# One message-passing kernel: who multiplies the first of four groups of edge values, ScalarE or VectorE

## The reference, cut to what matters

```
qi = Q[src]; kj = K[dst]
score = (qi * kj).sum(-1) + 0.1 * (edge_attr * qi[:, :RBF]).sum(-1) + logm[dst]
smax = segment_max(score, src)
es = exp(minimum(score - smax[src], 20.0))
denom = segment_sum(es, src)
alpha = es / (denom[src] + 1e-10)
m = h[dst] @ Wm[i]
aggi = segment_sum(alpha[:, None] * m, src)
```

## Time and profile before

| | us |
|---|---|
| median of 3 runs (5575.12, 5592.55, 5577.47) | 5577.47 |
| the profiled execution | 5589.14 |
| its span from the first to the last instruction | 5587.4 |
| around the span | 1.7 |
| `attend` in the third layer, from the first `keys` (3018.2) to the end of the last `total` (3445.6) | 427.4 |
| `attend` in the fourth layer (3545.5 to 3974.6) | 429.1 |

### The profile page before, as it was taken

The page is one execution under the profiler, slowest core; times in us unless marked ns, Lnnn a source line. Parts: engine busy times, 40 slices in busy tenths (PEclk is TensorE's granted clock), DMA queues, the critical chain, the costliest instruction groups (busy, mean ns, idle before and its releaser), DMA issues. The chain is left out here.

```text
span 5587.4 us, 187942 instructions
## 1 busy us (share of the span) xinstructions
PE 4125.9 (74%) x78491; PEld 3524.3 (63%) x78576; DVE 3831.4 (69%) x8933; ACT 2701.2 (48%) x8154; POOL 2683.2 (48%) x2702
## 2 busy tenths in 40 slices
PE   6888885026666489859976996799477844977886
PEld 4455553015555389849975996699456823977786
DVE  6888875149999689849966986699584446436254
ACT  3333331026666479839974996599402424100410
POOL 2777777757666267717762774377222500000000
PEclk7666665559999699969986997899697976988897
DMA  9322222248777366436634662566166342000000
GB/s 355 81 74 74 69 67 68 57 95 210 193 198 207 101 171 178 134 87 171 175 106 113 181 172 67 154 175 176 32 123 212 136 145 86 2 10 4 4 4 11
DMA packets 537236, 653.08 MB, mean 117 GB/s; under 512 B 321984, under 2 KB 369220, under 8 KB 533141
## 3 DMA queue, kind: packets, MB, share of 16 engines
q1 hardware_dynamic: 499989, 591.11, 38.0%
q0 software_dynamic: 33856, 48.44, 3.7%
q10 hardware_dynamic: 2496, 0.98, 0.1%
HBM read 460.24 MB, written 180.09 MB: 115 GB/s over the span
## 5 line engine op out<-in xcount | busy, mean ns | idle before, releaser
L299 POOL DMA_INDIRECT edges<-sb_bk_rec,sb_bk_pos x782 | 785.9, 1005 | 324.4 <-issue 234.1
L1749 ACT ACTIVATE sb_at_val<-banks,sb_at_prob 128x49 f32<-128x49 f32 x3800 | 783.0, 349 | 42.9 <-PE banks L1674 36.5
L1797 DVE CUSTOM_DVE_ANT_0 sb_at_left<-banks,sb_at_others 128x512 f32<-128x512 f32 x1000 | 644.9, 660 | 108.9 <-PE banks L1655 93.6
L1634 PE MATMUL banks<-sb_near,sb_at_hotT_d 128*128 128x49 bf16 x11100 | 617.8, 185 | 28.9 <-DVE sb_at_key L1774 10.6
L1636 PE MATMUL banks<-sb_queryp,sb_at_hotT_s 128*128 128x49 bf16 x11400 | 633.5, 186 | 5.6 <-issue 5.5
L1634 PEld LDWEIGHTS banks<-sb_near,sb_at_hotT_d 128*128 128x128 fp8e4 x11100 | 565.1, 97 | 35.9 <-issue 28.7
L1636 PEld LDWEIGHTS banks<-sb_queryp,sb_at_hotT_s 128*128 128x128 fp8e4 x11400 | 565.2, 96 | 6.7 <-issue 6.0
L1594 POOL TENSOR_TENSOR sb_at_key<-sb_at_key,sb_at_attr 128x400 f32<-128x400 f32 (+1 forms) x400 | 374.1, 936 | 371.9 <-ACT sb_at_key L1722 350.4
L1732 ACT ACTIVATE sb_at_others<-sb_at_hotT_s,sb_at_minus_big 128x1536 bf16<-128x1536 fp8e4 (+2 forms) x400 | 534.7, 1337 | 3.9 <-DVE sb_at_tops L1797 3.9
L1601 POOL TENSOR_TENSOR sb_at_val<-sb_at_val 128x490 f32<-128x490 f32 (+1 forms) x400 | 387.5, 969 | 67.3 <-ACT sb_at_val L1749 65.8
L1674 PE MATMUL banks<-sb_near,sb_at_hotT_d 128*128 128x49 bf16 x11100 | 364.6, 186 | 51.2 <-ACT sb_at_val L1749 32.2
(11 more groups left out here) (696 smaller groups left out, 10284.1 us busy)
## 6 DMA issues: line engine op xcount, KB each, us to landing
edges<-sb_pad SPq DMA_DIRECT2D x95, 460.0 KB, 7.2
sb_gt_rec<-edges SPq DMA_DIRECT2D x25, 1748.0 KB
sb_at_attr<-attr SPq DMA_DIRECT2D x100, 400.0 KB, 3.4
sb_at_attr<-attr SPq DMA_DIRECT2D x100, 360.0 KB, 4.0
sb_at_hot_s<-rows_src SPq DMA_DIRECT2D x100, 320.0 KB, 3.7
sb_we_hotT<-rows_dst_t SPq DMA_DIRECT2D x52, 592.0 KB, 5.8
sb_at_hotT_s<-rows_src_t SPq DMA_DIRECT2D x96, 320.0 KB, 3.3
sb_at_hotT_d<-rows_dst_t SPq DMA_DIRECT2D x96, 320.0 KB, 3.2
```

The lines of the kernel that those rows point to most:

```text
L299: pool.indirect_dma_start(list1, bass.IndirectOffsetOnAxis(pos[:, t:t + 1], 0), rec[:, k, j, :], None).then_inc(sent[k], 16)
L1634: pe.matmul(ps[:, 0, H1 * j:H1 * j + H1], where, what, start=(n == 0), stop=(n == 2))
L1749: ins = act.mul(val[:, v % VB, j, 0, :], ps[:, 5, H1 * j:H1 * j + H1], prob[:, i % 2, k:k + 1])
L1797: dve.tensor_tensor_reduce(left[:, x % 2, 0:n], ps[:, 3 + x % 2, 0:n], others[:, w % 2, ks[0] - first:ks[-1] + 1 - first, :].rearrange("p ...
```

## The change

A new helper on DVE weighs the first group of each block (10 slots) in one instruction, right before `scores` in the step in which ACT used to do it. ACT's `weigh` returns at once for q = 0. Since two engines now weigh, the count of weighed groups is held by two semaphores, and every wait for it becomes a helper, `weighed`, that waits for both: on PE ahead of every `values`, on POOL ahead of every `remainders`, on ACT ahead of the exponential.

```diff
+        def weighed(eng, v):
+            if v:
+                eng.wait_ge(s_val0, -(-v // Q))
+            if v - -(-v // Q):
+                eng.wait_ge(s_val, v - -(-v // Q))
...
             def remainders(v):
...
-                pool.wait_ge(s_val, v + 1)
+                weighed(pool, v + 1)
...
             def values(i, q):
                 v = Q * i + q
-                if v:
-                    pe.wait_ge(s_val, v)
+                weighed(pe, v)
...
             def weigh(i, q):
                 v = Q * i + q
                 if q == 0:
+                    return
+                if q == 1:
                     act.wait_ge(s_prob, i + 1)
...
+            def weigh(i):
+                v, n = Q * i, len(TAKE[0])
+                dve.wait_ge(s_prob, i + 1)
+                dve.wait_ge(s_h, v + 1)
+                if v >= VB:
+                    dve.wait_ge(s_sum, v - VB + 1)
+                dve.tensor_tensor(val[:, v % VB, 0:n, 0, :], ps[:, 5, 0:H1 * n].rearrange("p (j f) -> p j f", f=H1),
+                                  bc(prob[:, i % 2, 0:n], H1), ALU.mult).then_inc(s_val0, 1)
...
+                if 0 <= u - LAG - 1 < U and (u - LAG - 1) % Q == 0:
+                    weigh((u - LAG - 1) // Q)
                 if 1 <= u <= U:
                     scores(*divmod(u - 1, Q))
```

More of the change, by code:

```diff
@@ L1522, in attend @@
     names = ["keys", "rowk", "key", "dot", "score", "split", "turned", "rows", "laid", "top", "max", "mgot", "shift", "prob",
-             "h", "val", "rest", "split2", "sum", "added", "link", "minus", "others"]
+             "h", "val", "rest", "split2", "sum", "added", "link", "minus", "others", "val0"]
     rings = [f"attr{k}" for k in range(2)] + [f"hots{k}" for k in range(2)] + [f"hotT{k}" for k in range(HT)] + [
@@ L1528, in attend @@
             block, s_keys, s_rowk, s_key, s_dot, s_score, s_split, s_turned, s_rows, s_laid, s_top, s_max, s_mgot, s_shift,
-            s_prob, s_h, s_val, s_rest, s_split2, s_sum, s_added, s_link, s_minus, s_others, *dmas):
+            s_prob, s_h, s_val, s_rest, s_split2, s_sum, s_added, s_link, s_minus, s_others, s_val0, *dmas):
         s_attr, s_hots, s_hotT, s_far = dmas[0:2], dmas[2:4], dmas[4:4 + HT], dmas[4 + HT:8 + HT]
+        def weighed(eng, v):
[3 more added lines that the diff above has]
+                eng.wait_ge(s_val, v - -(-v // Q))
         @block.sync
@@ L1737, in probs @@
                 if i >= 2:
-                    act.wait_ge(s_val, Q * (i - 1))
+                    weighed(act, Q * (i - 1))
                 act.activation(prob[:, i % 2, :], shift[:], ACT.Exp).then_inc(s_prob, 1)
```

## The result

The changed kernel takes **5628.72 us** (median of 6 runs, 5615.97 to 5644.51), the kernel before in the same set of runs 5585.56 (5575.12 to 5592.55). The ratio is **1.0074, 95% interval [1.0057, 1.009]**: 41 us slower, with 32 to 50 as bounds (the two medians are 43 apart). The forecast was 5568.5 with a range to 5616; the measured time lies above that range. The kernel before came out 8 us higher in these six runs than in the three that the forecast started from, but 41 us on that lower base would give 5619, still above the range. In size the change is that of the rival "the race for the port is lost" with all 51 near ties turned (+38).

The account below looks back on a forecast made before the run. The order within one block (15.39 us), led by PE's unbroken run, was taken as the bound. -6 us from the drain and -3 from `values` gave -9, hence 5568.5 us; range 5553 to 5616, the forecast alone 5555 to 5583.

Parts of the forecast that it names:

- the race for the port is lost: Rival, chance 0.34: POOL takes the shared SBUF port before DVE's second divide instruction; +6 us (17 blocks) to +38 (51).
- near ties: 51 of 100 blocks where DVE's second divide instruction starts only 0.01 to 0.06 ahead of POOL's key addition.
- The chain of a block: From one `maxima` to the next: PE, ACT's key copy, POOL's addition, DVE's divide and tops; 15.39 us in most blocks.
- ten multiplications less on ACT: 2.03 us per block removed where ACT's next copy waits for PE anyway: worth 0 in mid-layer.
- the addition covered: DVE's added work fits into waits and 0.57 slack; the rival, not covered, costs 0.37 to 0.59 a block, chance 0.07.
- DVE's new instruction: 128x490 ahead of `scores`: 0.67, net 0.59 after overlap; delays the first divide instruction's start by 0.37.
- The price of `values`: In q = 3 PE no longer waits for ACT: 0.04 to 0.05 in some 60 of 100 blocks, about -3 us.
- few races lost: The forecast's own case, chance 0.48: change hidden but for the drain, POOL seldom first at the port.
- The price of a lost race: DVE's third divide instruction ends 0.86 later on the chain; such blocks last 16.2.
- The second waits: Second semaphore on 400 waits each of PE and POOL: 0 to 0.07 each, taken as 0.
- The drain: Behind a layer's last keys, PE waits less for ACT: 2.0 less 0.5 for waits, 1.5 a layer, -6 us in four.
- the first of the two savings: In the drain, `values` of group 93 waited 1.11 for ACT; DVE, at most one top later, saves 0.8.

Follow-up runs that it names:

- dve_extra: Kernel before plus one more VectorE instruction of 128x490 (result unused) where the change puts its own; ScalarE still weighs all groups, old waits: 5597.92 us, 1.0006.
- after_single_2: Changed kernel with one wait in place of two for the weighed values, run again on chip A: 5609.34 us, 1.0025 against the kernel before.
- after_again: The changed kernel run once more, on chip A in the fourth set: 5620.74 us, 1.005 against the kernel before.
- first pair: The changed kernel against the kernel before in the original measurement: 5628.72 against 5585.56 us, ratio 1.0074.
- second pair: The changed kernel and the kernel before, both run once more on chip A in the fourth set: 5620.74 and 5597.72 us.
- after_single: Changed kernel with one wait in place of two for the weighed values, on chip B: 5832.62 us, 0.9985 against the kernel before.

## Why the prediction was wrong, point by point

- **The chain of a block** (15.39) holds, though "most blocks have that length" does not: of 76 blocks in mid-layer 31 take 15.30 to 15.45, and their mean is 15.83. Only what was on it moved the time: ten multiplications less on ACT were worth nothing in mid-layer, as said, and dve_extra shows the addition covered.
- **DVE's new instruction:** taken at 0.67 and 0.59 net, it measured 0.66 and delays what follows by 0.58. L1793 starts 0.26 later behind `maxima` (11.38 to 11.64; forecast 0.37) and ends where it did, with POOL.
- **The price of `values`:** `keys` were to come 0.04 to 0.05 earlier; the key copy came 0.04 earlier. This step was right in size, and its use was wrong: it was booked as a gain of 3 us, and the race as lost in few blocks, 17 of them at least if it came to that. **This is the step that failed.** By the forecast's own numbers 31 of the 51 near ties had a margin of 0.04 or less and 19 one of 0.05, so 0.04 to 0.05 less leaves nearly all at zero or within 0.01 of it or below. It called 17 sure, about 20 even, and gave "few races lost" 0.48 against 0.34. The median margin was 0.04, so the median came out at zero or below: 41 more blocks blocked in one execution, 20 in another, at 0.86 each 35 and 17 us. In the undisturbed near ties the margin went, in nanoseconds, from 47 to -6: the copy came 38 earlier, and the divide's second instruction 13 later. The second part nobody had booked. The same start differs by 6 between two executions of the kernel before, so it can't be said what makes it.
- **The price of a lost race**, 0.86, holds: L1794 at 1.02, L1795 at 0.92, blocks of 16.2 to 16.3 where 16.2 was named.
- **The second waits** were taken at zero with 0 to 0.07 as bounds, for the engine that waits. As a delay of POOL they are 0.01 at most: its subtraction starts 11.11 behind `maxima` instead of 11.10. In the kernel as a whole they cost 23 us on chip B with no race, and after_single_2 below after_again on chip A (1.0025 to 1.005) agrees. That term was mis-sized: it was looked for in a start time alone. Where the time goes is open.
- **The drain** was to give 1.5 a layer. From the last `maxima` to the end of the last `total` of the third layer:

```profile
3425.00 0.49 PEld L1664 LDWEIGHTS banks<-sb_at_mparts,sb_at_hotT_s 128*128 128x128 fp8e4 x17 [1.17 <-DVE sb_at_mparts L1810]
...
3444.96 0.59 PEld L1685 LDWEIGHTS banks<-sb_at_val,sb_at_hot_s 128*128 128x128 fp8e4 x9 [0.77 <-POOL sb_at_val L1603]
```

```profile
3446.30 0.81 PEld L1671 LDWEIGHTS banks<-sb_at_mparts,sb_at_hotT_s 128*128 128x128 fp8e4 x29 [1.17 <-DVE sb_at_mparts L1818]
...
3464.28 0.59 PEld L1691 LDWEIGHTS banks<-sb_at_val,sb_at_hot_s 128*128 128x128 fp8e4 x9 [2.20 <-POOL sb_at_val L1610]
```

  20.55 before, 18.57 after: 2.0 less, and 1.6 in the fourth layer. But the first of the two savings did not come. The `values` at 3440.55, which answers to 3419.38, still waits 1.27, now for VectorE, whose weighing stood behind two tops (L1805); I had allowed for one:

```profile
3438.30 0.69 DVE L1805 CUSTOM_DVE_ANT_0 sb_at_left<-banks,sb_at_others 128x512 f32<-128x512 f32 x1
...
3439.22 0.69 DVE L1805 CUSTOM_DVE_ANT_0 sb_at_left<-banks,sb_at_others 128x512 f32<-128x512 f32 x1 [0.22 <-PE banks L1662]
...
3439.83 0.66 DVE L1834 TENSOR_TENSOR sb_at_val<-banks,sb_at_prob 128x490 f32<-128x490 f32 x1
```

- **The sum** of the first pair: 35 for the race, 14 for second waits (0.0025 between after_again and after_single_2, an interval that reaches from 2 to 26 us), some 7 off for the drain: 42, measured 41 [32, 50]. That it fits so well is in part luck. The 41 blocks are those of the profiled execution, the fastest of the six, which is only 26.9 us longer than the one of the kernel before. In it the four stretches from a layer's first `maxima` to its last take 33.2 more (1542.1 against 1508.9), which the race alone fills, and with drains and the starts of the layers the stage takes 20.9 more (2005.9 against 1985.0). In the second pair it is 19.9 more (1998.1 against 1978.2) with 20 more blocks lost: 17 for these, 7 off for the drains, which leaves some 10 for second waits. So the traces show a loss of 20 us in the stage, most or all of it the race; what the rest of the 41 is no trace shows.

## What to carry to other kernels

A margin is a number to be priced like any other: where two engines meet at a resource within hundredths of a microsecond, every step that shifts one of them by as much decides it, also a step that only removes work, and the result then differs by chip and by execution. Don't trust a cheap forecast there; order the two engines by a semaphore, which here gained 0.6% in the kernel before on one chip and 0.4% on another, and take out the waits that an earlier wait has covered. When testing such a theory, shift the margin from both sides (two matmuls more, two fewer): it costs least and tells most.

## What the runs showed of the hardware that was not expected

- Who holds the port is decided to the hundredth, by who starts first. Over the twelve kernels of the table, near ties with a margin of -0.02 or less were blocked in 79 of 79 cases, of -0.01 in 56 of 72, of 0.00 in 12 of 75, of 0.01 and more in none. In nanoseconds the line is sharper still: with POOL ahead by 7 or more 131 of 131 were blocked, by 6 15 of 18, by 5 1 of 5, by 4 or less or behind none of 570. A blocked instruction ended 49 to 61 ns after POOL's in all 1963 cases of the three instructions of the divide.
- Two chips run the same program with PE at different pace inside one group of 54 matmuls: 1.45 to 1.55 instead of 1.40 in 75 of 179 groups of after_single on chip B, in 1 of 185 of after_single_2 on chip A, at the same granted clock. With it went the sign of a change: single waits gave 0.9985 on one and 1.0025 on the other. What these 0.08 are is open.
- PE stops for no reason that the profile names, 67 to 109 times in 76 blocks, for 0.15 (the shortest that is listed) to 1.8 each, 0.5 to 0.85 a block. From one stop to the next it is a multiple of 126 weight loads, give or take two, in 84 of 93 cases in after_again and in 36 of 70 in the kernel before.
- Second waits that are already met, 788 of them, cost POOL 0.01 at most in its start, and the kernel 0.004 on chip B (0.0017 to 0.0063).
